# Expert tiles of a mixture-of-experts layer: from 25 full and 11 mixed to 33 full and 3 mixed

## The reference, cut to what matters

```python
def experts(x, cond, rms_w, wg_W, wg_b, gg_W, gg_b, W1, b1, W2, b2, W3, b3):   # 8 experts, 2 for each token
    xn = rms_w * (x * rsqrt(mean(x * x) + 1e-6))
    gate_w = softmax(xn @ wg_W + wg_b + (cond @ gg_W + gg_b))
    topk_w, topk_i = top_k(gate_w, 2)
    cw = sum(one_hot(topk_i, 8) * topk_w)
    h1 = relu(einsum('bsh,ehm->bsem', x, W1) + b1)       # 256 -> 512
    h2 = relu(einsum('bsem,emn->bsen', h1, W2) + b2)     # 512 -> 512
    out_e = einsum('bsen,enh->bseh', h2, W3) + b3        # 512 -> 256
    return einsum('bseh,bse->bsh', out_e, cw)
```

## Time and profile before

| | us |
|---|---|
| median of three runs (784.91 to 787.38) | 785.79 |
| the profiled execution | 789.31 |
| its span, first to last instruction | 787.6 |
| PE busy | 747.4 |
| DVE busy | 515.8 |
| ACT busy | 296.3 |

### The profile page before, as it was taken

How to read it: one execution, slowest core, us unless ns; L and a number is a source line. 1 busy time by engine, 2 the same in 40 slices (tenths; PEclk the granted TensorE clock), 3 DMA queues, 4 the chain that set the end, 5 groups by cost and what they waited for, 6 DMA issues and landing times.

```text
span 787.6 us, 22268 instructions
## 1 busy us (share of the span) xinstructions
PE 747.4 (95%) x9218; PEld 598.1 (76%) x9218; DVE 515.8 (65%) x1101; ACT 296.3 (38%) x823; POOL 98.5 (13%) x111
## 2 busy tenths in 40 slices
PE   6389999999999999999999999999999999999786
PEld 3289998544449999868778977887788789778675
DVE  3846665666654445245778777877786787778756
ACT  3032221233432221236345633653464356345420
POOL 2121112433421100110000000000000000000000
PEclk9599999999999999999999999999999999999989
DMA  9778211332315203200000000000000100000000
GB/s 317 275 259 294 92 41 55 98 102 83 104 45 192 91 29 107 79 25 22 23 29 8 23 28 23 15 23 28 22 10 29 28 11 21 29 14 9 8 10 15
DMA packets 30865, 53.45 MB, mean 68 GB/s; under 512 B 3563, under 2 KB 19307, under 8 KB 30253
## 3 DMA queue, kind: packets, MB, share of 16 engines
q1 hardware_dynamic: 20432, 32.47, 12.2%
q0 software_dynamic: 5024, 14.69, 6.5%
q10 hardware_dynamic: 5309, 4.87, 1.9%
HBM read 45.19 MB, written 6.82 MB: 66 GB/s over the span
## 4 chain that ended last, share of the span: by engine, by line
PE 88%; DMA 4%; DVE 3%; issue 2%; SPq 1%; ACT 1%; DVEq 0%
PE ps L828 15%; PE ps L729 11%; PE ps L854 7%; PE ps L913 7%; PE ps L761 6%; PE ps L699 5%; PE ps L723 5%; PE ps L879 4%; DMA arena<-in_w 4%; PE ps L933 3%; PE ps L749 3%; PE ps L693 2%; PE ps L904 2%; PE ps L872 2%; PE ps L964 2%
## 5 line engine op out<-in xcount | busy, mean ns | idle before, releaser
L828 PE MATMUL ps<-arena,l_weights 128*128 128x128 f32 x1024 | 125.8, 277 | 1.6 <-issue 1.6
L828 PEld LDWEIGHTS ps<-arena,l_weights 128*128 128x128 f32 x1024 | 119.3, 192 | 2.9 <-issue 1.8
L729 PE MATMUL ps<-h_t,w_now 128*128 128x128 f32 x800 | 93.6, 275 | 1.4 <-DVE h_t L1588 1.0
L729 PEld LDWEIGHTS ps<-h_t,w_now 128*128 128x128 f32 x800 | 91.3, 192 | 1.9 <-issue 1.8
L1222 ACT ACTIVATE arena<-ps,cols 128x128 f32<-128x128 f32 x256 | 72.9, 370 | 19.8 <-PE ps L828 19.8
L596 POOL DMA_INDIRECT arena<-expert_out,slot_of x32 | 30.2, 945 | 359.1 <-DVE arena L1614 311.4
L1151 ACT ACTIVATE h_t<-ps,cols 128x128 f32<-128x128 f32 x100 | 28.4, 366 | 121.2 <-issue 102.7
L1563 DVE COPY w_now<-arena 128x2048 f32 x25 | 30.8, 1231 | 57.7 <-PE ps L729 50.5
L1256 ACT ACTIVATE arena<-arena 128x256 f32<-128x256 f32 x16 | 6.7, 416 | 147.1 <-DVE arena L1753 147.1
L854 PE MATMUL ps<-l_weights,arena 128*64 128x512 f32 x256 | 61.8, 604 | 0.0
L913 PE MATMUL ps<-l_weights,arena 128*128 128x256 f32 x256 | 58.3, 381 | 0.1
(11 more groups left out here) (294 smaller groups left out, 1311.7 us busy)
## 6 DMA issues: line engine op xcount, KB each, us to landing
arena<-in_w SPq DMA_DIRECT2D x16, 512.0 KB
arena<-in_w SPq DMA_DIRECT2D x8, 1024.0 KB
expert_out<-y ACTq DMA_DIRECT2D x36, 128.0 KB
arena<-in_x_t SPq DMA_DIRECT2D x2, 1024.0 KB, 6.3
arena<-in_x SPq DMA_DIRECT2D x16, 128.0 KB, 2.6
out<-arena SPq DMA_DIRECT2D x16, 128.0 KB, 1.7
b<-in_b SPq DMA_DIRECT2D x1, 1024.0 KB, 12.9
l_weights<-in_wq SPq DMA_DIRECT2D x1, 1024.0 KB
```

What stands on the lines that cost most here:

```text
L729: last = mm(ps[:, 2, m * P:(m + 1) * P], w2_now[:, k, m * P:(m + 1) * P], h1_t[j % 2][:, k, :], start=k == 0, stop=k == KM - 1)
L828: last = mm(ps[:, b, c * P:(c + 1) * P], wt[:, k, f:f + P], m_t[:, k, :], start=k == 0, stop=k == KH - 1)
```

## The change

`FULL` is set to 33 and `MIXED` follows as 3, so there are still 36 tiles. A rest of over 64 rows now makes a whole block of 128 (an expert's count is raised by 63 and cut to a multiple of 128); a rest of 1 to 64 rows makes a unit. Blocks fill full tiles from the front; a unit goes to a full tile that no block uses, as long as there is room, and to a mixed tile otherwise. With `small` experts that have a unit, `units_left` gives 4, 5, 4, 5, 4, 5, 5, 6, 6 units for 0 to 8 of them, so 3 mixed tiles hold all. `HOST` is 28, the number of blocks that there are at least: full tiles from 28 on may hold a unit.

The order by position: 0 to 7 as before; 8 to 12 are the tiles 28 to 32; 13 to 15 mixed; 16 to 35 the tiles 8 to 27. `tile_expert` is made in two parts: for the first 8 tiles ahead of the first one, for the others in the piece of the set-up for j = 1, and PE, ACT and DVE wait for that (`experts_set`, 2) at position 8. The diff, cut to its core:

```diff
-FULL = -(-(TOPK * TOK - EXP * (P - 1)) // P)
-MIXED = -(-(TOPK * TOK - FULL * P + EXP * (UNIT - 1) - (UNIT - 1)) // P)
+FULL = 33
+def units_left(small):
+    blocks = (TOPK * TOK + (EXP - small) * (UNIT - 1) - small) // P
+    return UNITS * max(blocks - FULL, 0) + max(small - max(FULL - blocks, 0), 0)
+MIXED = -(-max(units_left(small) for small in range(EXP + 1)) // UNITS)
+HOST = -(-(TOPK * TOK - EXP * UNIT) // P)
-FIRST_MIXED = EXP + 5
+FIRST_MIXED = EXP + FULL - HOST
 def slot_tile(p):
-    return FULL + nth(p) if mixed(p) else nth(p)
+    if p < EXP:
+        return p
+    if p < FIRST_MIXED:
+        return HOST + p - EXP
+    return FULL + nth(p) if mixed(p) else nth(p) - (FULL - HOST)
...
# layer3 (PE); relu1 (ACT) and take_w1 (DVE) alike
-                n = nth(j)
-                e = pe.value_load(tile_expert[0:1, n:n + 1], min_val=0, max_val=EXP - 1)
+                n, tile = nth(j), slot_tile(j)
+                if j == EXP:
+                    pe.wait_ge(experts_set, 2)
+                e = pe.value_load(tile_expert[0:1, tile:tile + 1], min_val=0, max_val=EXP - 1)
...
# slots (DVE), ahead of the first tile
-            step(tt(count_i, incl[:, :, TT - 1], first_row, ALU.subtract))
-            step.go(ts(full_i, count_i, -P, None, ALU.bitwise_and))
-            step(ts(up_i, count_i, float(UNIT - 1), None, ALU.add))
+            step(stt(up_i, incl[:, :, TT - 1], float(UNIT - 1), first_row, ALU.add, ALU.subtract))
+            step.go(ts(full_i, up_i, -P, None, ALU.bitwise_and))
+            step(ts(count_i, up_i, -UNIT, None, ALU.bitwise_and))
             step.go(ts(seg_of[0], full_i, float(P), None, ALU.min))
-            step(ts(up_i, up_i, -UNIT, None, ALU.bitwise_and))
+            step(tt(seg_of[2], count_i, full_i, ALU.subtract))
             step.go(tt(seg_of[1], full_i, seg_of[0], ALU.subtract))
-            step(tt(seg_of[2], up_i, full_i, ALU.subtract))
-            step.go(dve.tensor_tensor_scan(seg_ends, seg, ...))
+            step(tt(rank, ps[:, 2, 0:TT * EXP]..., excl..., ALU.add))
+            step.go(dve.tensor_tensor_scan(starts, seg, ...))
             step.go(tt(past_full, full_i, first_row, ALU.add))
-            step.go(ts(past_first, first_row, float(P), None, ALU.add))
-            step(tt(rank, ps[:, 2, 0:TT * EXP]..., excl..., ALU.add))
-            step.go(tt(seg_from, seg_ends, seg, ALU.subtract))
+            step(ts(past_first, first_row, float(P), None, ALU.add))
+            step.go(ts(room, blocks_end, -1.0 / UNITS, float(FULL * UNIT), ALU.mult, ALU.add))
...
+            step.go(stt(behind, start_of[2], blocks_end, room.to_broadcast([P, EXP]), ALU.subtract, ALU.min))
...
+            step.go(stt(start_of[2], behind, 0.0, start_of[2], ALU.max, ALU.add))
...
# tile_expert, ahead of the first tile: 8 tiles against 24 starts, not 25 tiles against 16 ends
-            step(tt(ends_le[0:1], seg_ends[0:1, 0:2 * EXP]...([1, FULL, 2 * EXP]), bc(tile_start[0:1, :], 2 * EXP), ALU.is_le))
+            step(tt(starts_le[0:1, 0:EXP], starts[0:1, 0:3 * EXP]...([1, EXP, 3 * EXP]),
+                    bc(tile_start[0:1, 0:EXP], 3 * EXP), ALU.is_le))
             dve.wait_ge(ids_ps, 1)
             dve.tensor_copy(slot_tok[:, :], bank(0, SLOT_TILES)).then_inc(ids_set, 1)
-            step(red(segment_f[0:1, :], ends_le[0:1], X, ALU.add))
-            step(dve.tensor_copy(segment[0:1, :], segment_f[0:1, :]))
-            ts(tile_expert[:, :], segment[0:1, :], EXP - 1, None, ALU.bitwise_and).then_inc(experts_set, 1)
+            step(red(segment_f[0:1, 0:EXP], starts_le[0:1, 0:EXP], X, ALU.add))
+            step(ts(segment[0:1, 0:EXP], segment_f[0:1, 0:EXP], -1.0, None, ALU.add))
+            ts(tile_expert[:, 0:EXP], segment[0:1, 0:EXP], EXP - 1, None, ALU.bitwise_and).then_inc(experts_set, 1)
...
# side_stage, j == 1 (DVE)
-                    step(tt(row_ends_le, seg_ends...([P, MIXED, 3 * EXP]), bc(row_slot, 3 * EXP), ALU.is_le))
-                    step(red(row_segment, row_ends_le, X, ALU.add))
-                    step(dve.tensor_copy(row_expert[:, :], row_segment))
+                    rest = slice(EXP, FULL)
+                    step.go(tt(starts_le[0:1, rest], starts[0:1, 0:3 * EXP]...([1, FULL - EXP, 3 * EXP]),
+                               bc(tile_start[0:1, rest], 3 * EXP), ALU.is_le))
+                    step(tt(row_starts_le, starts[:, 0:3 * EXP]...([P, MIXED, 3 * EXP]), bc(row_slot, 3 * EXP), ALU.is_le))
+                    step.go(red(segment_f[0:1, rest], starts_le[0:1, rest], X, ALU.add))
+                    step(red(row_segment, row_starts_le, X, ALU.add))
+                    step.go(ts(segment[0:1, rest], segment_f[0:1, rest], -1.0, None, ALU.add))
+                    step(ts(row_expert[:, :], row_segment, -1.0, None, ALU.add))
+                    ts(tile_expert[:, rest], segment[0:1, rest], EXP - 1, None, ALU.bitwise_and).then_inc(experts_set, 1)
                     ts(row_expert[:, :], row_expert[:, :], EXP - 1, None, ALU.bitwise_and).then_inc(row_expert_set, 1)
```

More of the change, by code:

```diff
@@ L238, in build @@
         past_first, past_full, to_first, to_full, to_rest, jump = (r(EXP) for _ in range(6))
-        seg, seg_from = r(3 * EXP), r(3 * EXP)
+        seg, room, behind = r(3 * EXP + 1), r(1), r(EXP)
         rank, over_first, over_full = (r(TT, EXP) for _ in range(3))
@@ L269, in build @@
         w_amax, w_scale, w_inv = r(KH, NBLK), r(KH, NBLK), r(KH, NBLK)
-        seg_ends, row_slot, row_segment = r(3 * EXP), r(MIXED), r(MIXED)
-        row_ends_le = r(MIXED, 3 * EXP)
+        starts, row_slot, row_segment = r(3 * EXP + 1), r(MIXED), r(MIXED)
+        starts_le, row_starts_le = r(FULL, 3 * EXP), r(MIXED, 3 * EXP)
+        tile_start = r(FULL)
+        segment_f, segment = r(FULL), r(FULL).bitcast(I32)
         y_shift = [r(TOPK, TT) for _ in range(2)]
@@ L1143, in relu1 @@
                     return
-                n = nth(j)
-                e = act.value_load(tile_expert[0:1, n:n + 1], min_val=0, max_val=EXP - 1)
+                tile = slot_tile(j)
+                if j == EXP:
+                    act.wait_ge(experts_set, 2)
+                e = act.value_load(tile_expert[0:1, tile:tile + 1], min_val=0, max_val=EXP - 1)
                 act.wait_ge(l1_ps, j + 1)
@@ L1412, in _ @@
             step(dve.memset(scan_zero, 0.0))
+            step(dve.memset(seg[:, 0:1], 0.0))
             dve.wait_ge(cond_ps, 1)
@@ L1454, in _ @@
             step(tt(excl, incl, tot, ALU.subtract))
-            first_row, seg_of = excl[:, :, 0], [seg[:, n * EXP:(n + 1) * EXP] for n in range(3)]
-            from_of = [seg_from[:, n * EXP:(n + 1) * EXP] for n in range(3)]
-            step(tt(count_i, incl[:, :, TT - 1], first_row, ALU.subtract))
-            step.go(ts(full_i, count_i, -P, None, ALU.bitwise_and))
-            step(ts(up_i, count_i, float(UNIT - 1), None, ALU.add))
+            first_row, seg_of = excl[:, :, 0], [seg[:, n * EXP + 1:(n + 1) * EXP + 1] for n in range(3)]
@@ L1461, in _ @@
+            start_of, blocks_end = [starts[:, n * EXP:(n + 1) * EXP] for n in range(3)], starts[:, 2 * EXP:2 * EXP + 1]
+            step(stt(up_i, incl[:, :, TT - 1], float(UNIT - 1), first_row, ALU.add, ALU.subtract))
+            step.go(ts(full_i, up_i, -P, None, ALU.bitwise_and))
+            step(ts(count_i, up_i, -UNIT, None, ALU.bitwise_and))
             step.go(ts(seg_of[0], full_i, float(P), None, ALU.min))
-            step(ts(up_i, up_i, -UNIT, None, ALU.bitwise_and))
+            step(tt(seg_of[2], count_i, full_i, ALU.subtract))
@@ L1463, in _ @@
             step.go(tt(seg_of[1], full_i, seg_of[0], ALU.subtract))
-            step(tt(seg_of[2], up_i, full_i, ALU.subtract))
-            step.go(dve.tensor_tensor_scan(seg_ends, seg, scan_zero.rearrange("p e i -> p (e i)")[:, 0:3 * EXP], 0.0, ALU.add, ALU.add))
+            step(tt(rank, ps[:, 2, 0:TT * EXP].rearrange("p (i e) -> p i e", e=EXP), excl.rearrange("p e i -> p i e"), ALU.add))
+            step.go(dve.tensor_tensor_scan(starts, seg, scan_zero.rearrange("p e i -> p (e i)")[:, 0:3 * EXP + 1], 0.0, ALU.add, ALU.add))
@@ L1466, in _ @@
             step.go(tt(past_full, full_i, first_row, ALU.add))
-            step.go(ts(past_first, first_row, float(P), None, ALU.add))
-            step(tt(rank, ps[:, 2, 0:TT * EXP].rearrange("p (i e) -> p i e", e=EXP), excl.rearrange("p e i -> p i e"), ALU.add))
-            step.go(tt(seg_from, seg_ends, seg, ALU.subtract))
+            step(ts(past_first, first_row, float(P), None, ALU.add))
+            step.go(ts(room, blocks_end, -1.0 / UNITS, float(FULL * UNIT), ALU.mult, ALU.add))
+            step.go(stt(to_full, start_of[1], -float(P), start_of[0], ALU.add, ALU.subtract))
@@ L1470, in _ @@
+            step.go(tt(to_first, start_of[0], first_row, ALU.subtract))
+            step.go(tt(to_rest, full_i, start_of[0], ALU.add))
             step(tt(over_first, rank, per_e(past_first), ALU.is_ge))
```

(21 more changed lines are left out.)

11 lines of the change are left out of this document (5 added, 6 removed).

## The result

The median of five runs after the change is 776.05 us (774.46 to 777.57), beside 786.03 us (784.91 to 787.38) for five of the kernel before: a ratio of 0.9875, with a 95% interval of 0.9858 to 0.9893. The profiled execution took 777.57 us.

The account below looks back on a forecast made before the run. PE alone was taken to set the pace in both kinds of tile. Eight tiles gave 10.1 us less, the chain 0.05 more; from the median, 785.79 - 10.1 = 775.7 us, range 773.2 to 779.0.

Parts of the forecast that it names:

- The eight tiles: 8 mixed tiles become full ones, 8.57 us against 7.31 each on PE: 10.1 us gained, all on the path.
- the difference is the turnings: Mixed against full tile: of 1.26 us, 1.12 for the two turnings, 0.14 small change around the smaller matmuls.
- The serial chain: Slots ahead of the first tile: one small operation added, wide `rank` sum moved; between -0.1 and +0.2 us, taken as 0.05.
- The first part of `tile_expert`: Comparison shrinks from 400 to 192 elements, costing 0.34 us; off the path, so 0, at best -0.4.
- The cover at position 1: Set-up piece gets 1.5 us more DVE work, ending about 66.1; 2 us left before PE asks, so cost 0.
- Position 8's wait: New wait for `experts_set` 2 at position 8, on work some 50 us earlier: 0.
- the order of the tiles: Positions 8 to 12 take tiles 28 to 32 instead of 8 to 12; no new load is waited for: 0.
- the attention loads: SP's four loads of attention weights come some 70 us earlier, again beside full tiles: 0.
- The start eats a part: Rival: added DVE work reaches PE (1.5 us), small matmuls ahead of the first tile slow by 1.9; 779.1 us; chance 0.04.
- No gain: Rival: something other than PE holds each new full tile at 8.57 us, or tiles become 37; 785.8 us; chance 0.02.
- Narrow matmuls lose: Rival: 128-column matmuls at 275 ns each without overlap make a full tile 15.1 us; 838 us; chance 0.01.
- Slower by the clock: Rival: PE's clock stays at 1.2 GHz into full tiles, 7.3 us more each; 798 us with three tiles; chance 0.03.

Follow-up runs that it names:

- e11_after_third: The changed kernel, unaltered, run again in the third group of runs beside its own runs of the kernel before: 775.75 us, 0.9860 of before.

## Why the prediction was right, point by point

**The eight tiles: right.** 8 x 1.26 = 10.1 us. Both periods came out to 0.01 us, and the runs with 29 and 35 full tiles moved by 5.06 and 5.75 us where the two periods say 5.04 and 6.05. That the forecast hit the median to 0.35 us is in part luck: the interval of the gain is 8.4 to 11.2 us.

**That the difference is the turnings: right in the place, incomplete in the price.** The runs that cut them show that their cost isn't in proportion to their number, and that about half of the 1.26 stays with a quarter of them. The forecast didn't need that.

**The serial chain: right in sign, mis-sized within its bounds.** I took 0.05 us, within -0.1 and +0.2. PE's wait for it went from 10.28 to 10.41 us: 0.13, and the same 10.28 or 10.29 in both profiles of before, 10.41 or 10.42 in those of after and its variants with 36 tiles. The first layer 1 came 0.51 later (42.96 for 42.45), over the 0.3 that I had named as a sign of a wrong step. 0.30 of that is there at 22.05 and 22.35 us, ahead of the chain that the change touches, and the 64 small matmuls took 0.07 more (5.48 for 5.41). Both vary from run to run, as told below, so the sign was set too tight to mean anything.

**The first part of `tile_expert`: right.** 192 elements cost 0.34, off the path.

**The cover at position 1: right that it holds, wrong in its length.** "2 us are left" is the term that failed. The piece ended where I put it (66.13), but with everything 0.5 us later, so that this agreement is luck. So it had grown by 1.1 and not 1.5. The copy did not follow at once but started at 67.01 (66.5 without the late start, for 66.1 forecast): 0.87 us stand between the piece and W1's copy in after and in each run with more work there. In before I had read all of the 1.26 us as a wait for weights that the piece could eat into. And the row that decides isn't L713 but the L743 behind it, whose relu2 queues behind both copies on DVE. The runs with two and four comparisons more put the cover up to that row at 1.2 us. Another piece of the size of the added one (1.1) would just about have used it up.

**Position 8's wait, the order of the tiles, the attention loads: 0, right.** The run with the loads 58 us later than after shows no difference for the loads. PE's timeline shows no idle time at position 8 in after.

**The sum.** Against the profiled execution I gave a span of 777.5; it is 775.8, 1.7 less, while the medians agree to 0.35 us. The profile's surplus over the eight tiles is known in places. The 0.4 us on the way into attention come back in every comparison; why, stays open. The 0.59 at the entry and the 0.56 behind the small matmuls vary from run to run. Where the 0.56 are, ACT does two exponentials ahead of a copy that PE's next group waits for, in both kernels alike; they begin 2.43 us behind the start of PE's small matmuls in before and 1.23 in after. What sets that wasn't tried. The last 446 us vary as well: from that group to the end are 447.0 us in before and 446.3 to 447.1 in the versions of after. That the median didn't show these is inside the spread of the runs, 3 us wide.

**The rivals.** *The start eats a part*: the piece reached PE with nothing; the clock around the small matmuls did vary (5.48 for 5.41 us), in both kernels alike. Its 779.1 us lies just above the range's end of 779.0, so the cases outside should have held 0.10 and not 0.06. *No gain* fell with the periods, and *37 tiles* with the 1056 records of layer 2, which are 33 full tiles, and the 24 of each half of the pairs, which are 3 mixed ones. *Narrow matmuls lose* fell too: a full tile's layer 2 of 32 records takes 3.57 us (302.77 to 306.34), 112 ns each, as before. *Slower by the clock* did not happen, but its mechanism is real: six more comparisons made a gap of 3.28 us, the clock fell, and the tile lost 2.5 us beyond the gap. It came back within about one tile, so by this one gap it would not have turned the sign.

## What to carry to other kernels

Where one engine is busy for all of a stretch, read the period of each kind of work by start to start of the same group, and price a change of mix by the difference of two periods; the periods held here to 0.01 us each, and their difference within 0.3 us for counts of 29, 33 and 35 full tiles. Before you call added work covered, look for the last instruction in its engine's queue that somebody waits for, not the next one, and ask whether the idle time behind it shrinks when the work grows: here 2 us of cover were 1.2. Test the cover by adding a known amount two or three times over: what was added less what was lost gives its length, read in the stage itself where the whole run spreads by more, and a larger step shows what the loss sets off.

## What the runs showed of the hardware

**A start that varies with the lengths of matmuls.** In thirteen profiles, of both kernels and the variants, layer 2 of the first tile starts anywhere from 46.19 to 48.93 us. Part of the spread is there 20 us earlier, in the small fp32 matmuls of the gate. Two of their groups in after, and the first of them again in the run with six comparisons more:

```profile
5.71 1.94 PE L632 MATMUL ps<-arena 66*32 66x512 f32 x8 [1.53 <-POOL arena L570]
...
13.13 1.05 PE L645 MATMUL ps<-arena 128*32 128x512 f32 x8
```

```profile
5.71 1.06 PE L632 MATMUL ps<-arena 66*32 66x512 f32 x8 [1.53 <-POOL arena L570]
```

Both start at 5.71; one takes 1.94 us for eight matmuls and the other 1.06, and the mask's matmul (L665) comes at 22.35 in the one and 19.85 in the other. Within after, too, the eight of L645 take 1.94 us at 9.76 and 1.05 at 13.13. The granted clock reads 1.00 in both up to 14 us, so that row doesn't show it; the lengths, apart by a factor of 1.8, look like the two levels of the clock, but that isn't shown. From that matmul on, the wait for the chain is the same to 0.01 us. The rest of the spread is in the 64 small matmuls ahead of the first tile: 5.48 us in after, 3.75 in `e11_after_third`, where the mean granted clock from 36 to 42 us was 0.63 and 0.96. A start that moves by 2.7 us from run to run is larger than every small term of this change; only the wait for the chain, read by itself, shows one of them.

**A single turning isn't a quarter of four.** In the stream one fp32 turning takes 0.21 to 0.26 us and four take 0.53 to 0.59.
